# The last node's keys for the 18 rounds that always run, loaded in one transfer at the head of the block

## The reference

```
h = (x_flat @ W_gat).reshape(M, HEADS, NUM_EXPERTS)
e = leaky_relu(a_src[src] + a_dst[dst], 0.2)
e_max = segment_max(e, dst);  ee = exp(e - e_max[dst])
denom = segment_sum(ee, dst); alpha = ee / (denom[dst] + 1e-16)
agg = segment_sum(h[src] * alpha[:, :, None], dst)
w = softmax(top_k(layernorm(agg).mean(heads), 2))
out = sum over experts of gate * (gelu(x @ W1 + b1) @ W2 + b2)
```

## Time and profile before

| | us |
|---|---|
| median of 3 runs | 4398.14 (4394.29 to 4399.58) |
| profiled execution, its time | 4400.41 |
| profiled execution, its span | 4398.5 |
| PE busy, share of the span | 2938.8, 67% |
| DVE busy | 2992.7, 68% |
| ACT busy | 1543.2, 35% |
| POOL busy | 1333.3, 30% |

### The profile page before, as it was taken

One profiled execution on the slowest core, in us unless ns is written; L12 is line 12 of the kernel. 1 busy time (PEld: TensorE's weight loads), 2 busy tenths in 40 slices (PEclk: granted clock), 3 DMA queues, 4 the chain that ended last, 5 costly groups with the idle time before them and its releaser, 6 DMA issues. The chain is left out here.

```text
span 4398.5 us, 30087 instructions
## 1 busy us (share of the span) xinstructions
PE 2938.8 (67%) x9220; PEld 1502.9 (34%) x9220; DVE 2992.7 (68%) x4591; ACT 1543.2 (35%) x2215; POOL 1333.3 (30%) x1388
## 2 busy tenths in 40 slices
PE   4888899799999998999656334544554553554019
PEld 1333344344444443433226222322222232232019
DVE  6999858787888786986754545654654664565465
ACT  1222225444444454445434123323322322332117
POOL 0000000000000000000002477777777777777600
PEclk8888899899999999999875567766776776777559
DMA  4111322364645454645757311111111111111237
GB/s 144 58 58 53 127 94 81 107 189 131 183 140 177 145 170 144 188 135 177 251 192 219 58 27 49 42 37 44 46 37 44 46 37 37 34 18 17 23 127 287
DMA packets 342679, 458.36 MB, mean 104 GB/s; under 512 B 83156, under 2 KB 257110, under 8 KB 333688
## 3 DMA queue, kind: packets, MB, share of 16 engines
q1 hardware_dynamic: 296760, 416.46, 29.2%
q0 software_dynamic: 45760, 40.00, 5.7%
HBM read 342.80 MB, written 113.51 MB: 104 GB/s over the span
## 5 line engine op out<-in xcount | busy, mean ns | idle before, releaser
L1449 POOL DMA_INDIRECT got<-scratch_tab,src_at x1280 | 1223.1, 956 | 390.1 <-issue 378.5
L587 PE MATMUL in_ps<-xT,w_in 128*128 128x512 f32 x2048 | 936.7, 610 | 4.4 <-issue 4.4
L1396 PE MATMUL hid_ps<-tokens,w 128*128 128x512 f32 x512 | 316.6, 751 | 862.1 <-ACT hid L1615 841.8
L546 POOL MEMSET w_in<- 1x128 int32 x1 | 0.2, 195 | 2064.2 <-PE in_ps L587 2064.2
L587 PEld LDWEIGHTS in_ps<-xT,w_in 128*128 128x128 f32 x2048 | 393.9, 196 | 484.4 <-issue 484.4
L604 PE MATMUL out_ps<-w_out,act 128*128 128x512 f32 x1024 | 472.9, 608 | 68.1 <-issue 35.9
L899 DVE TENSOR_TENSOR keys<-keys 128x1024 f32<-128x1024 f32 x380 | 464.2, 1222 | 10.7 <-ACT keys L713 9.5
L900 DVE TENSOR_TENSOR keys<-keys 128x1024 f32<-128x1024 f32 x380 | 464.0, 1221 | 0.0
L1544 DVE TENSOR_TENSOR hold<-by_value,is_loop 128x256 f32<-128x256 f32 x20 | 8.5, 426 | 631.1 <-ACT by_value L1626 631.1
L1396 PEld LDWEIGHTS hid_ps<-tokens,w 128*128 128x128 f32 x512 | 108.8, 236 | 956.6 <-ACT hid L1615 851.7
L1626 ACT ACTIVATE by_value<-got 128x1536 f32<-128x1536 f32 x20 | 80.6, 4028 | 771.6 <-DMA got<-scratch_tab,src_at 771.6
(11 more groups left out here) (267 smaller groups left out, 4078.0 us busy)
## 6 DMA issues: line engine op xcount, KB each, us to landing
w_out<-in_m_WoutT SPq DMA_DIRECT2D x256, 512.0 KB, 4.6
w_in<-in_m_WinT SPq DMA_DIRECT2D x128, 512.0 KB, 4.0
scratch_y<-ys SPq DMA_DIRECT2D x25, 1024.0 KB, 4.0
got<-scratch_tab,src_at POOLq DMA_INDIRECT x1280
xT<-scratch_xt SPq DMA_DIRECT2D x8, 2048.0 KB, 10.0
scratch_sz<-zst SPq DMA_DIRECT2D x64, 256.0 KB, 5.3
gz<-scratch_sz SPq DMA_DIRECT2D x64, 256.0 KB, 5.0
tokens<-scratch_y SPq DMA_DIRECT2D x16, 1024.0 KB, 9.3
```

The source lines that it names most:

```text
L587: last = t_.matmul(in_ps[:, z, :], w_in[:, n % WIN, k, :], xT[:, s % 2, k, :], start=(k == 0), stop=(k == KC - 1))
L1396: last = t.matmul(hid_ps[:, f], w1[:, e, f * P:(f + 1) * P], tokens[:, g * QW:(g + 1) * QW], start=True, stop=True)
L1449: g.indirect_dma_start(got[:, y, t, :], None, tab_d[:, :], bass.IndirectOffsetOnAxis(ap=src_at[:, y, t:t + 1], axis=0))\
```

## The change

A new tile `b_first` holds 1216 keys a partition, 19 counts of 64. POOL loads it once, right after the first `load_keys`, by one indirect DMA (`load_first_last`, semaphore `s_last`). The 19 counts of the always-run rounds read slices of it, and their rounds issue no `load_last`. The rounds of the loop still do. `merge` no longer waits for the last node's keys; the first `count` does. `merge` moves `b_pos` and `b_at` on only once, by 1216, before the loop, and then as before.

To make room, `same` is halved, so that a count takes eight parts of 16 nodes in place of four of 32. Since one read may now reach 1216 keys past the list's end, SP stores ten pads of 128 keys in place of one.

```
+FIRST_LAST = (2 * PAIRS + 1) * FR
+PADS = -(-FIRST_LAST // P)
...
-                        sp.dma_start(sorted_d[NE:NE + P, :].rearrange("(o c) x -> o (c x)", o=1),
-                                     pad).then_inc(s_stored, 16)
+                        for n in range(PADS):
+                            sp.dma_start(sorted_d[NE + n * P:NE + (n + 1) * P, :].rearrange("(o c) x -> o (c x)", o=1),
+                                         pad).then_inc(s_stored, 16)
...
-                g.wait_ge(s_stored, 32)
+                g.wait_ge(s_stored, 16 * PADS + 16)
...
+            b_first = sb("b_first", [P, FIRST_LAST], I32, st)
-            same = sb("same", [P, BINS // 4, FR], F32, st)
+            same = sb("same", [P, BINS // 8, FR], F32, st)
...
+                def load_first_last():
+                    g.indirect_dma_start(b_first[:], None, sorted_d[:, :],
+                                         bass.IndirectOffsetOnAxis(ap=b_at[:, 0:1], axis=0)).then_inc(s_last, 16)
...
-                load_last(0)
+                load_first_last()
-                def pair():
+                def pair(first):
                     for y in range(2):
                         g.wait_ge(s_idx, 1)
                         g.sem_clear(s_idx)
                         load_keys()
-                        load_last(1 - y)
+                        if not first:
+                            load_last(1 - y)
                         gather(y)
...
-                    v.wait_ge(s_key, 32 * r + 32)
+                    v.wait_ge(s_key, 16 * r + 16)
...
-                    v.tensor_copy(key_at[:], row_pos[:])
-                    ck(v.tensor_scalar(b_pos[:], b_pos[:], float(FR), float(NE), ALU.add, ALU.min))
-                    ck(v.tensor_copy(b_at[:], b_pos[:]))
+                    ck(v.tensor_copy(key_at[:], row_pos[:]))
+                    if last_on:
+                        ck(v.tensor_scalar(b_pos[:], b_pos[:], float(last_on), float(NE), ALU.add, ALU.min))
+                        ck(v.tensor_copy(b_at[:], b_pos[:]))
                     v.sem_inc(s_idx, 1)
...
-                    part = BINS // 4
+                    part = BINS // 8
...
-                merge(ck, 0, 0)
-                count(ck, 0)
+                merge(ck, 0, 0, 0)
+                v.wait_ge(s_last, 16)
+                count(ck, b_first[:, 0:FR])
```

More of the change, by code:

```diff
@@ L1285, in program @@
         s_key = sem("s_key")
+        s_last = sem("s_last")
         s_idx = sem("s_idx")
@@ L1441, in load_keys @@
                                          bass.IndirectOffsetOnAxis(ap=key_at[:, 0:1], axis=0)).then_inc(s_key, 16)
+                def load_first_last():
+                    g.indirect_dma_start(b_first[:], None, sorted_d[:, :],
+                                         bass.IndirectOffsetOnAxis(ap=b_at[:, 0:1], axis=0)).then_inc(s_last, 16)
                 def load_last(y):
                     g.indirect_dma_start(b_k[:, y], None, sorted_d[:, :],
-                                         bass.IndirectOffsetOnAxis(ap=b_at[:, 0:1], axis=0)).then_inc(s_key, 16)
+                                         bass.IndirectOffsetOnAxis(ap=b_at[:, 0:1], axis=0)).then_inc(s_last, 16)
                 def gather(y):
@@ L1472, in _ @@
                 for _ in range(PAIRS):
-                    pair()
+                    pair(True)
                 n = rounds(g)
                 with g.Fori(0, n):
-                    pair()
+                    pair(False)
                 g.wait_ge(s_block, 1)
@@ L1482, in _, with merge @@
             def _(v):
-                def merge(ck, r, y):
-                    v.wait_ge(s_key, 32 * r + 32)
+                def merge(ck, r, y, last_on):
+                    v.wait_ge(s_key, 16 * r + 16)
                     v.tensor_copy(lo_at[:, y], next_lo[:])
@@ L1505, in merge, with count @@
                     ck(v.tensor_tensor(row_pos[:], row_pos[:], n_edge[:], ALU.add))
-                    v.tensor_copy(key_at[:], row_pos[:])
-                    ck(v.tensor_scalar(b_pos[:], b_pos[:], float(FR), float(NE), ALU.add, ALU.min))
-                    ck(v.tensor_copy(b_at[:], b_pos[:]))
+                    ck(v.tensor_copy(key_at[:], row_pos[:]))
+                    if last_on:
+                        ck(v.tensor_scalar(b_pos[:], b_pos[:], float(last_on), float(NE), ALU.add, ALU.min))
+                        ck(v.tensor_copy(b_at[:], b_pos[:]))
                     v.sem_inc(s_idx, 1)
-                def count(ck, y):
-                    part = BINS // 4
-                    key = b_k[:, y].bitcast(F32).unsqueeze(1).to_broadcast([P, part, FR])
+                def count(ck, keys):
+                    part = BINS // 8
+                    key = keys.bitcast(F32).unsqueeze(1).to_broadcast([P, part, FR])
                     for n in range(0, BINS, part):
@@ L1581, in _, with pair @@
                 v.wait_ge(s_reset, 1)
-                merge(ck, 0, 0)
-                count(ck, 0)
+                merge(ck, 0, 0, 0)
+                v.wait_ge(s_last, 16)
+                count(ck, b_first[:, 0:FR])
                 v.sem_clear(s_mch)
-                def pair(i):
+                def pair(r, first):
                     ck = Chain(v, s_mch)
                     for y in range(2):
-                        merge(ck, 2 * i + y + 1, 1 - y)
-                        count(ck, 1 - y)
+                        if first:
+                            merge(ck, r + y + 1, 1 - y, FIRST_LAST if r + y + 1 == 2 * PAIRS else 0)
+                            count(ck, b_first[:, (r + y + 1) * FR:(r + y + 2) * FR])
+                        else:
+                            v.wait_ge(s_last, 16 * (r + y + 1) - 16 * (2 * PAIRS - 1))
+                            merge(ck, r + y + 1, 1 - y, FR)
+                            count(ck, b_k[:, 1 - y])
                         compute(ck, y)
@@ L1594, in _ @@
                 for i in range(PAIRS):
-                    pair(i)
+                    pair(2 * i, True)
                 with v.Fori(0, rounds(v)) as i:
-                    pair(i + PAIRS)
+                    pair(2 * i + 2 * PAIRS, False)
             @block.scalar
@@ L1870, in _ @@
                                             ALU.add).then_inc(s_fin, 1)
-SCRATCH = (("sorted", (NE + P, 1), I32), ("first", (P, 1), F32), ("len", (3, P), F32),
+SCRATCH = (("sorted", (NE + PADS * P, 1), I32), ("first", (P, 1), F32), ("len", (3, P), F32),
            ("sums", (P * TR, OUTS), F32), ("r", (B, C, S), F32), ("sz", (NJ, P, QW), F32), ("xt", (NI, P, KC, QW), F32),
```

## The result

The changed kernel took 4372.18 us (median of 6 runs, 4368.56 to 4379.66), the kernel before 4398.86 us (6 runs, 4394.29 to 4401.42). The ratio is 0.9942, with a 95% interval of 0.9930 to 0.9954: 26.7 us less, 4374 having been forecast. The profiled execution was the slowest of the six, 4379.66 us with a span of 4377.8, so it shows 20.7 us less than that of before.

The account below looks back on a forecast made before the run. The prediction took POOL's queue alone to set the 20 rounds: 22.5 us from 18 dropped loads plus 1.8 us at the head, with DVE and SP at zero, gave 4398.14 - 24.3 = 4373.8 us, range 4369 to 4382.

Parts of the forecast that it names:

- The bound: Third block: POOL's queue alone sets the 20 rounds of 84.55 us, until about 31 us are gone per round.
- The slots: Always-run rounds on POOL: 18 loads fewer at 1.25 us each, 22.5 us gained, rounds of 83.30 us.
- The large load: Third block's head: the 1216-key load holds POOL 1.02 us, between 0.94 and 1.28, at no cost.
- the stalled head: Rival, third block's head: the 622 KB load delays first gathers by up to 9.5 us, 4383.3 us; 5 in 100.
- The head: Third block's start: first merge waits for `edge_k` only and is shorter, so POOL starts 1.8 us sooner.
- DVE: Rounds: a count takes 20.0 us, 1.4 more, hidden in 31.44 us of idle time; cost zero.
- SP: Sorted list's store: nine more pads delay SP's queue 3.0 us, covered by a 4.5 us wait; cost zero.
- Paced gathers: Rival, rounds: DMA engines pace the gathers, so only the head gains, 4396.3 us; 5 in 100.
- the slowed gathers: Rival, rounds: the finer count slows gathers beside it by 0.4 us each, 4407 to 4502 us; 4 in 100.

Follow-up runs that it names:

- e10: The kernel of e9 with a second 64-key load, which nobody reads, in each of the 18 always-run rounds: 4418.19 us, ratio 1.0041.
- e8: The changed kernel with the first ordinary key load and first merge moved into the second block, and the third block's memsets moved to DVE: 4356.80 us, ratio 0.9905.
- e12: The changed kernel itself, unaltered, measured once more: 4374.71 us, ratio 0.9933.
- e11: The kernel before with the count in eight parts, ten pads and every last-node load 608 keys wide: 4399.81 us, ratio 0.9995.
- e5: The changed kernel with the first merge waiting for the 1216-key load too: 4377.59 us, ratio 0.9953.
- e9: The kernel before with only the count changed, to eight parts of 16 nodes: 4397.20 us, ratio 0.9991.
- e6: The changed kernel with 40 pads in place of ten: 4391.19 us, ratio 0.9983.
- e1: The kernel before with ten pads in place of one: ratio 1.0015, on a chip where the kernel before took 5078.37 us.
- e4: The same kernel as e11, on the chip of e1: ratio 1.0047.
- e7: The changed kernel with POOL issuing the head's two key loads before its iotas and memsets: 4371.05 us, ratio 0.9938.

## Why the prediction was right

*The bound.* On the chips on which the kernel takes about 4400 us, POOL's queue alone sets the rounds. Shown: by the unchanged waits after, by e10 (18 slots more, 21 us more) and by e8 (16.8 us off the head of the queue, 13.7 to 15.4 us off the time).

*The slots.* 18 x 1.25 = 22.5 us were forecast; the rounds became 22.7 us shorter. Rounds of 83.30 us were forecast, 83.29 came, and 83.39 in e12. That 22.5 and 22.7 agree so closely is luck, since two traces of the changed kernel differ by 2 us there. The slot itself is no luck: the 18 spare loads of e10 took 22.5 us on POOL.

*The large load.* Its time on POOL was taken as 1.02 us between 0.94 and 1.28; it was 0.942. Width does not count there up to 1216 keys, and e11 agrees with 946 ns at 608 keys. The bound from above came from the loads of 4096 keys, which take 1.12 to 1.28 us, and a rise in proportion to the width between the two was wrong, by less than 0.1 us. The load landed after 7.5 us, at 2469.6, before the first count wanted it, so the stalled head did not occur.

*The head.* 1.8 us were forecast, 1.84 came, and the guess that the longest landing of its line is the first one's held (2460.84 to 2466.99). e5 gives 2.75 us of it back, more than the 1.5 counted for the wait, since the large load lands later than the small one did.

*DVE.* 20.0 us a count were forecast, 20.07 measured; hidden. The wait at the head of `compute` was forecast at 29 us and is 28.4. e9 shows the finer count harmless by itself.

*SP.* 3.0 us of stores forecast, 3.2 measured, covered. But the cover was thinner than reckoned. Of 4.5 us only 0.4 were left, where 1.5 should have been: the landing of `scratch_first` that SP waits for was longer too, 14.4 us from its issue to SP's next transfer against 13.5 before. e6 shows what lies behind it.

*The rivals.* Paced gathers fell with e10 and e11; the slowed gathers with e9, mean 956 ns as before. What the forecast did not have is the dependence on the chip. On the chip of e1 to e4 another engine sets the rounds, and the finer count, which was costed at zero, came with 29 us more for a reason that is open. The changed kernel itself did not run there, so whether it gains on that chip is open too.

## What to carry to other kernels

Find the queue that never waits, and count its slots, not its share of busy time: an indirect load cost the same slot here from 64 to 1216 keys a partition, so one wide load can take the place of many small ones for the price of one, where their places are known beforehand. Then look at what such a queue does before its first useful item; here 16.8 us of loads, memsets and a merge at the head were worth 13.7 to 15.4 us, against 22.5 for the 18 slots. A cost that is hidden is hidden by a certain wait on a certain chip: the count's 1.5 us were free under 28 us of DVE's waiting, and the same edit came with 29 us more on a chip on which the rounds hang on something else. There, an agreement in size (20 times 1.5 us) was no proof; the idle time before `compute`, read from the trace, spoke against it.

## What the hardware showed unexpectedly

On one of the chips PE ran in jerks in part of the time in which POOL issued gathers, 2.5 us apart for matmuls of 0.37 us (read from e1, which has only nine pads more than the kernel before), and the kernel before took 5078 us in place of 4400, though e1's first two blocks ran at their usual length. The mean granted clock was 0.763 there in e1's profile and 0.808 in that of the kernel before; whether that is a cause or follows from the jerks was not tried, and neither was the cause of the jerks. An indirect load on POOL took 0.94 us for 64, 608 and 1216 keys a partition, and 1.12 to 1.28 us for 4096. A DVE instruction of 64 elements took 1.49 us in place of 0.30 beside a memset on POOL (e7, seen once).
